# Flamingo layer pair on one core: broadcast one-hots for the expert map, paired base adds without an awaited store, head normalisation on ScalarE and 16-bit gate selection

## What is computed

```python
# second block ("ffn"): 16 heads of width 64, 8 experts, two chosen for each token and head
w, sel = top_k(x @ Ws, 2); mix_v = sigmoid(w) on the chosen experts
v = mix_v * (x @ Wv);  attn = softmax(q k^T / 8) @ v
mask_o = one_hot(top_k(x @ Wd, 2)).sum();  out = einsum(mask_o, attn, Wo)
# fourth block ("moe"): 12 experts, three for each token
topw, sel = top_k(x @ Wg, 3);  cw = softmax(topw) on the chosen experts
h = gelu(x @ Wup[e] + bup[e]);  y = h @ Wdown[e] + bdown[e];  out = sum_e cw[e] * y[e]
```

## Time and profile before

| | us |
|---|---|
| median of 3 runs (lowest, highest) | 1533.5 (1526.81, 1538.6) |
| the profiled execution | 1535.35 |
| its span, first to last instruction | 1533.6 |
| `ffn_stage` in it | 305 to 821 |
| `route` in it | 1053.3 to 1133.3 |
| `run_experts` in it | 1133.3 to 1533.6 |

### The profile page before, as it was taken

The page is one execution under the profiler, slowest core; times in us unless marked ns, Lnnn a source line. Parts: engine busy times, 40 slices in busy tenths (PEclk is TensorE's granted clock), DMA queues, the critical chain, the costliest instruction groups (busy, mean ns, idle before and its releaser), DMA issues. The chain is left out here.

```text
span 1533.6 us, 35189 instructions
## 1 busy us (share of the span) xinstructions
PE 1313.0 (86%) x13822; PEld 1029.4 (67%) x13822; DVE 1180.1 (77%) x2235; ACT 853.8 (56%) x1815; POOL 276.9 (18%) x240
## 2 busy tenths in 40 slices
PE   2399999768898898998975999995379999999997
PEld 2266767546676676776753667764258899989996
DVE  2656767568999999999863577776949888888884
ACT  1256666325565555555641666664227676767672
POOL 2000000000000000000000000000015666666663
PEclk9958788579999999999976899995569999999999
DMA  7000000023424334335321000000548888888771
GB/s 217 11 5 9 5 5 2 1 52 80 125 72 111 107 87 115 87 85 136 94 61 33 8 6 9 1 1 2 171 136 251 235 242 237 242 237 238 232 210 31
DMA packets 172065, 152.96 MB, mean 100 GB/s; under 512 B 62589, under 2 KB 154386, under 8 KB 171906
## 3 DMA queue, kind: packets, MB, share of 16 engines
q1 hardware_dynamic: 151906, 129.51, 28.4%
q0 software_dynamic: 13936, 16.79, 5.7%
q10 hardware_dynamic: 6064, 4.46, 1.0%
HBM read 116.89 MB, written 36.70 MB: 100 GB/s over the span
## 5 line engine op out<-in xcount | busy, mean ns | idle before, releaser
L1826 POOL DMA_INDIRECT out<-m_yo,m_xg x70 | 161.1, 2301 | 138.2 <-DVE m_yo L1941 122.7
L1848 ACT ACTIVATE m_hf<-m_ps,m_bue 128x256 f32<-128x256 f32 x280 | 117.2, 471 | 106.5 <-PE m_ps L84 106.5
L1051 ACT ACTIVATE f_pr<-f_ps,f_nb 128x256 f32<-128x256 f32 x256 | 107.1, 472 | 104.3 <-DVE f_nb L1314 99.7
L82 PE MATMUL m_ps<-m_xt,m_us 128*128 128x256 f16 x560 | 153.8, 275 | 0.0
L83 PE MATMUL m_ps<-m_xt,m_us 128*128 128x256 f16 x560 | 153.7, 274 | 0.0
L84 PE MATMUL m_ps<-m_xt,m_us 128*128 128x256 f16 x560 | 153.7, 274 | 0.0
L82 PE MATMUL m_ps<-m_ds,m_hs 128*128 128x256 f16 x560 | 152.6, 273 | 0.3 <-DVE m_yo L1941 0.3
L84 PE MATMUL m_ps<-m_ds,m_hs 128*128 128x256 f16 x560 | 152.6, 273 | 0.0
L83 PE MATMUL m_ps<-m_ds,m_hs 128*128 128x256 f16 x560 | 152.6, 273 | 0.0
L690 DVE SCALAR_TENSOR_TENSOR x_pt<-x_ps,x_pt 120x512 f16<-120x512 f32 x128 | 88.3, 690 | 77.7 <-ACT x_pt L480 77.0
L472 ACT ACTIVATE x_pr<-x_ps,x_mx 128x120 f32<-128x120 f32 x512 | 142.8, 374 | 8.3 <-DVE x_mx L686 8.3
(11 more groups left out here) (364 smaller groups left out, 3894.3 us busy)
## 6 DMA issues: line engine op xcount, KB each, us to landing
m_uraw<-in_L_ffn_Wup SPq DMA_DIRECT2D x35, 1024.0 KB, 5.4
m_draw<-in_L_ffn_Wdown SPq DMA_DIRECT2D x35, 1024.0 KB, 5.6
head_values<-f_v_row SPq DMA_DIRECT2D x16, 520.0 KB, 5.4
f_vh<-head_values SPq DMA_DIRECT2D x16, 520.0 KB, 3.8
head_outputs<-f_at_row SPq DMA_DIRECT2D x16, 512.0 KB, 3.0
f_at_in_t<-head_outputs SPq DMA_DIRECT2D x16, 512.0 KB, 6.0
expert_values<-f_pv_row SPq DMA_DIRECT2D x8, 512.0 KB, 2.8
f_pv_in_t<-expert_values SPq DMA_DIRECT2D x8, 512.0 KB, 5.6
```

What stands on the lines that cost most here:

```text
L82: pe.matmul(out, lhs[0], rhs[0], start=(n == 0), stop=False)
L1051: ins = act.activation(pr[h % 2][:, ti, :], S(h)[:, ti, :], ACT.Exp, bias=nb[h % 2][:, ti:ti + 1])
L1826: pool.indirect_dma_start(rows_of, bass.IndirectOffsetOnAxis(xg[j % RING][:, ti, D:D + 1].bitcast(I32), 0), yo[j % 2][:, ti, :], None, bou ...
L1848: ins = act.activation(hf[:, q, m, :], U(q)[:, m, :], ACT.Gelu, bias=weights.bue[par][:, 2 * q + m:2 * q + m + 1], scale=UNSPLIT)
```

## The change

In `ffn_stage` the multiplication of `normalise` goes from VectorE, where it is one instruction for a pair of heads, to ScalarE, where it is four Copy activations of 128 x 64 with the reciprocal as scale, behind `exps` in the same odd step; VectorE keeps the reciprocal and signals `rs_done`. The tensors `hit` and `sel` become 16-bit, the second maximum has a 16-bit tensor `top_rank` of its own, and the ranks are copied once into 16 bits (`rank16`).

In `route` the 16-bit identity is made first, and the transposes wait for it alone; the running sum takes four shifted additions of all 12 experts; the three `picked` products become one; the one-hots are made by three groups of three broadcast instructions, whose last dimension is a pair, so that lanes, columns and row numbers are stored twice over; TensorE waits for a group of 16 choices; the base is made for two tiles at a time over four banks, with eight additions of 128 x 512 for sixteen of 128 x 256; and SyncE no longer waits for the store of the base.

```diff
@@ ffn_stage
-        hit = sb("hit", [P, TPB * GATES, E0])
-        sel = sb("sel", [P, TPB, 2, H, E0])
+        hit = sb("hit", [P, TPB * GATES, E0], F16)
+        sel = sb("sel", [P, TPB, 2, H, E0], F16)
+        rank16 = sb("rank16", [P, E0], F16)
...
+            def normalise(b, hp):
+                h = 2 * hp
+                act.wait_ge(rs_done, H // 2 * b + hp + 1)
+                for i in range(2):
+                    h8, x = at_head(h + i)
+                    for ti in range(TPB):
+                        ins = act.activation(at[:, ti, h8, x, :], O(h)[:, i, ti, 0:DH], ACT.Copy,
+                                             scale=rs[hp % 2][:, 2 * i + ti:2 * i + ti + 1])
+                ins.then_inc(o_done, 1)
...
                     if b < B:
                         exps(b, h)
+                    if h % 2 == 1:
+                        if h >= 5 and b < B:
+                            normalise(b, (h - 5) // 2)
+                        elif h < 5 and b >= 1:
+                            normalise(b - 1, (h - 5) // 2 + H // 2)
...
-                ranks = bcast_mid(s.rank[:, E1 - E0:E1], TPB * GATES)
+                ranks = bcast_mid(rank16[:], TPB * GATES)
...
-                chain(dve.reciprocal(r, O(h)[:, :, :, DH]))
-                dve.tensor_tensor(at[:, :, h8:h8 + 2, x, :].rearrange("p t h d -> p h t d"), O(h)[:, :, :, 0:DH],
-                                  r.unsqueeze(3).to_broadcast([P, 2, TPB, DH]), ALU.mult).then_inc(o_done, 1)
+                dve.reciprocal(r, O(h)[:, :, :, DH]).then_inc(rs_done, 1)
@@ route
+            chain(pool.tensor_copy(ident16[:], s.ident[:]))
             pool.memset(ones[:], 1.0)
...
-            sp.wait_ge(b_done, TILES)
+            sp.wait_ge(b_done, B)
             sp.dma_start(out.rearrange("b (t p) d -> p (b t) d", p=P), s.x[:]).then_inc(out_based, 16)
-            sp.wait_ge(out_based, 16)
...
-            pe.wait_ge(masks_made, 6)
+            pe.wait_ge(masks_made, 1)
...
-            for tile in range(TILES):
-                if tile % 4 == 0:
-                    pe.wait_ge(cwt_done, tile // 4 + 1)
-                if tile >= 2:
-                    pe.wait_ge(b_done, tile - 1)
-                pe.matmul(BASE(tile), cwt[:, tile * P:(tile + 1) * P], s.bdown[:],
-                          start=True, stop=True).then_inc(b_ready, 1)
+            for q in range(B):
+                if q % 2 == 0:
+                    pe.wait_ge(cwt_done, q // 2 + 1)
+                if q >= 4:
+                    pe.wait_ge(b_done, q - 3)
+                for ti in range(TPB):
+                    tile = TPB * q + ti
+                    last = pe.matmul(BASE(q)[:, ti, :], cwt[:, tile * P:(tile + 1) * P], s.bdown[:], start=True, stop=True)
+                last.then_inc(b_ready, 1)
...
-            chain(dve.tensor_copy(ends[:, 0:1], blocks[:, 0:1]))
-            for e in range(1, E1):
-                chain(dve.tensor_tensor(ends[:, e:e + 1], ends[:, e - 1:e], blocks[:, e:e + 1], ALU.add))
+            chain(dve.tensor_copy(sums[1][:, SHIFT:], blocks[:]))
+            for i, back in enumerate((1, 2, 4, 8)):
+                chain(dve.tensor_tensor(sums[i % 2][:, SHIFT:], sums[1 - i % 2][:, SHIFT:],
+                                        sums[1 - i % 2][:, SHIFT - back:SHIFT + E1 - back], ALU.add))
...
-            for n in range(CHOICES):
-                dve.tensor_scalar(lane_hot[:, n, :], lanes[:], lane_f[:, n:n + 1], None, ALU.is_equal)
-                ins = dve.tensor_scalar(column_hot[:, n, :], lanes[:, 0:COLUMNS], column_f[:, n:n + 1],
-                                        row_f[:, n % TILES:n % TILES + 1], ALU.is_equal, ALU.mult)
-                if n % HOT_GROUP == HOT_GROUP - 1:
-                    ins.then_inc(hot_ready, 1)
+            spread = lambda ap, k: ap.unsqueeze(2).to_broadcast([P, TILES, k, 2])
+            counting = lambda k: lanes[:, 0:2 * k].rearrange("p (k d) -> p k d", d=2).unsqueeze(1).to_broadcast([P, TILES, k, 2])
+            for r in range(TOP1):
+                group = slice(r * TILES, (r + 1) * TILES)
+                into = column_hot[:, group, :].rearrange("p n (k d) -> p n k d", d=2)
+                chain(dve.tensor_tensor(into, counting(COLUMNS // 2), spread(column_2[:, group, :], COLUMNS // 2), ALU.is_equal))
+                dve.tensor_tensor(lane_hot[:, group, :].rearrange("p n (k d) -> p n k d", d=2),
+                                  counting(P // 2), spread(lane_2[:, group, :], P // 2), ALU.is_equal)
+                dve.tensor_tensor(into, into, spread(row_2[:], COLUMNS // 2), ALU.mult).then_inc(hot_ready, 1)
...
-            for tile in range(TILES):
-                dve.wait_ge(b_ready, tile + 1)
-                dve.tensor_tensor(s.x[:, tile, :], s.x[:, tile, :], BASE(tile), ALU.add).then_inc(b_done, 1)
+            for q in range(B):
+                pair = slice(TPB * q, TPB * q + TPB)
+                dve.wait_ge(b_ready, q + 1)
+                dve.tensor_tensor(s.x[:, pair, :], s.x[:, pair, :], BASE(q), ALU.add).then_inc(b_done, 1)
```

More of the change, by code:

```diff
@@ L1346, in _ @@
             dve.wait_ge(made, 6)
+            chain(dve.tensor_copy(rank16[:], s.rank[:, E1 - E0:E1]))
             for j in range(FF_FRONT - 1):
@@ L1542, in route @@
         sb = lambda name, shape, dt=F32: prep.enter_context(nc.sbuf_tensor(t + name, shape, dt))
+        two = lambda name, shape, dt=F32: [sb(f"{name}{i}", shape, dt) for i in range(2)]
         xn = sb("xn", [P, TILES, WIDE])
@@ L1555, in route @@
         top = sb("top", [P, 3, TILES])
-        filled, blocks, ends = sb("filled", [P, E1], I32), sb("blocks", [P, E1]), sb("ends", [P, E1])
-        start = sb("start", [P, E1])
+        filled, blocks, sums = sb("filled", [P, E1], I32), sb("blocks", [P, E1]), two("sums", [P, SHIFT + E1])
+        ends, start = sums[1][:, SHIFT:SHIFT + E1], sb("start", [P, E1])
         slot_f, slot_i = sb("slot_f", [P, CHOICES]), sb("slot_i", [P, CHOICES], I32)
         lane_i, column_i = sb("lane_i", [P, CHOICES], I32), sb("column_i", [P, CHOICES], I32)
-        lane_f, column_f = sb("lane_f", [P, CHOICES]), sb("column_f", [P, CHOICES])
+        lane_2, column_2 = (sb(n, [P, CHOICES, 2], F16) for n in ("lane_2", "column_2"))
         lanes_i, lanes = sb("lanes_i", [P, P], I32), sb("lanes", [P, P], F16)
-        row_i, row_f = sb("row_i", [P, TILES], I32), sb("row_f", [P, TILES])
+        row_i, row_2 = sb("row_i", [P, TILES], I32), sb("row_2", [P, TILES, 2], F16)
         lane_hot = sb("lane_hot", [P, CHOICES, P], F16)
@@ L1584, in _ @@
             chain(pool.iota(lanes_i[:], [[1, P]], base=0, channel_multiplier=0))
-            pool.tensor_copy(row_f[:], row_i[:])
+            pool.tensor_copy(row_2[:], bcast(row_i[:], 2))
             chain(pool.tensor_copy(lanes[:], lanes_i[:]))
-            chain(pool.tensor_copy(ident16[:], s.ident[:]))
             pool.iota(nth[:], [[1, NB]], base=0, channel_multiplier=0)
             pool.memset(xn[:, :, D + META:WIDE], 0.0)
+            for i in range(2):
+                pool.memset(sums[i][:, 0:SHIFT], 0.0)
             pool.iota(token[:], [[P, TILES]], base=0, channel_multiplier=1)
@@ L1741, in _ @@
             chain(dve.tensor_copy(blocks[:], filled[:]))
[L1742 to L1745 removed]
+            chain(dve.tensor_copy(sums[1][:, SHIFT:], blocks[:]))
+            for i, back in enumerate((1, 2, 4, 8)):
+                chain(dve.tensor_tensor(sums[i % 2][:, SHIFT:], sums[1 - i % 2][:, SHIFT:],
+                                        sums[1 - i % 2][:, SHIFT - back:SHIFT + E1 - back], ALU.add))
+            chain(dve.tensor_tensor(start[:], ends, blocks[:], ALU.subtract))
             chain(dve.scalar_tensor_tensor(place[:], bcast_mid(start[:], TILES), float(BT), RANK, ALU.mult, ALU.add))
[L1747 to L1748 removed]
+            chain(dve.tensor_tensor(picked[:].rearrange("p r t e -> p r (t e)"), chosen[:].rearrange("p r t e -> p r (t e)"),
+                                    bcast_mid(place[:].rearrange("p t e -> p (t e)"), TOP1), ALU.mult))
             chain(dve.tensor_reduce(slot_f[:], picked[:].rearrange("p r t e -> p (r t) e"), AX_X, ALU.add))
```

43 lines of the change are left out of this document (20 added, 23 removed).

## The result

The changed kernel takes 1484.61 us in the median (1481.57 to 1492.49, 4 runs) against 1530.15 us of the kernel before on the same chip: a ratio of 0.9706, with a 95% interval of 0.9641 to 0.9772. The forecast was 1491 us, faster: 42.4 us less than before, where the medians here are 45.5 apart. The profiled execution took 1487.02 us, with a span of 1485.3 us, 48.3 us less than the span before.

What follows compares the result with a forecast made beforehand. VectorE was taken to bound seven elements of `ffn_stage`, and `route` to be a chain; 22.4 us from `route` plus 20 from `ffn_stage`, 42.4 in all, took the median from 1533.5 to 1491 us, range 1472 to 1512.

Steps and rivals of the forecast that it cites:

- The rival in which TensorE takes over: `ffn_stage`: TensorE becomes the limit, only heavy steps give, some 8 us left there, 1503 us in all; chance 0.14.
- the one in which ScalarE paces every odd step: `ffn_stage`: `normalise` on ScalarE delays `pt_part` and TensorE in odd steps; 19 us slower, 1552 us; chance 0.02.
- First transposes: `route`: with the identity made first, TensorE's transposes start earlier, -1.1 us.
- Running sum: `route`: a copy and four additions instead of a copy and 11, 1.0 us for 2.3, -1.3.
- Products: `route`: three products of 192 values become one of 576, 0.76 us, -0.4; twice-stored lanes and columns give 0.1 back.
- One-hots: `route`: 96 VectorE instructions of 17.9 us become three groups of 2.6, 7.8 in all, -10.1 us.
- More products behind the last group: `route`: TensorE has 16 products left behind the last one-hot group instead of 8, +0.5 us.
- Base: `route`: four banks let TensorE go on, -2.1 us; the wider last addition costs 0.3; together -1.8.
- Store: End of `route`: without SyncE's wait for the base's store the experts start 8.3 us earlier, 0.5 left for the barrier.
- Store ordering: Experts: block 2's weights queue behind the store; cost 0, up to 8.3 us if late, rival 1499 us, chance 0.08.
- `ffn_stage`: Moved multiplication and 16-bit gates relieve VectorE of 4.3 us an element; 2.9 come through, times seven, 20 us; drain 0.
- Comparisons in 16 bits: `ffn_stage`: two comparisons of 16-bit ranks with one broadcast value gain 0; by the other reading 4 us more.

Runs made afterwards that it cites:

- e3: The changed kernel with SyncE's wait for the base's store put back; 1489.76 us, ratio 0.9751.
- e7: The changed kernel with a second 2 MB store, into a tensor nothing reads, behind the base's in SyncE's queue; 1487.66 us, ratio 0.9776.
- e4: The changed kernel with the 96 single one-hot instructions and groups of eight back; 1491.62 us, ratio 0.9754.
- e8: The changed kernel with four of eight base products ahead of the map's, six banks, and four additions ahead of VectorE's first weight split; 1482.68 us, ratio 0.9726.
- e2: The changed kernel with the multiplication of the heads back on VectorE, 16-bit gates kept; 1490.39 us, ratio 0.9759.
- e10: e5 with the heads of the last batch element alone normalised on VectorE; 1476.52 us, ratio 0.9662.
- e9: e8 with mask spreads one step later as in e5 and the third block's gathers moved from `route` to the experts' stage; 1469.53 us, ratio 0.9632.
- e6: The changed kernel with each of the four activations of a pair made twice on ScalarE, the copy never read; 1495.23 us, ratio 0.9795.
- e5: The changed kernel with VectorE's two mask spreads in steps 8 and 9 instead of 7 and 8; 1478.81 us, ratio 0.9708.

## Why the prediction was right

**The bound.** That VectorE paces the full elements held: relieved of 4.3 us it gave 3.29, and it is still the fullest engine. The rival in which TensorE takes over (8 us of gain in the stage) fell; the stage gave 20.6. So did the one in which ScalarE paces every odd step: one step in an element gave back 0.37 us.

**First transposes,** -1.1: they now start 2.67 us after the stage's first instruction instead of 3.43, so -0.8, and VectorE's halves release them. **Running sum,** -1.3: from its copy to `start` 1.02 instead of 2.33, -1.3. **Products,** -0.4: 0.79 instead of 1.18 us, -0.4; the doubled lanes and columns cost 0.04, not 0.1. **One-hots,** -10.1: 7.75 instead of 17.9, -10.1. **More products behind the last group,** +0.5: 1.21 us of waiting instead of 0.74, +0.5. The map's copy came at 42.3 us instead of 54.4, -12.1 against -12.3.

**Base,** -1.8: from the map's copy to the store's issue 14.67 instead of 16.93, -2.3. The 32 products took 14.02 us in one piece, 0.44 each, at the clock of 0.50 that the earlier trace rows had; more of them in a row did not raise it. **Store,** -8.3: 1.45 instead of 9.17, -7.7, and 6.96 in e3. This is the term that was a little too large: I left 0.5 us for the handover, and it is 1.45, so the sign that the first block comes within 1 us of the store's issue was missed. `route` as a whole: -22.0 against -22.4.

**Store ordering,** 0: no DMA wait at block 2's split. I had called it a draw at 12 us, and the load landed 10.5 us after the first block, 0.6 us before ScalarE wanted it. The forecast's limit was too late: in e7 the split at 15.0 us already costs 2.9, so the cost begins nearer 12.

**`ffn_stage`,** -20: -20.6, in part by luck, and by another road in three places. Of the light steps with a pair of heads, 9, 11 and 13 let all of VectorE's gain through (0.47, 0.48 and 0.48 us shorter), 15 and 1 a part (0.13 and 0.34), and only step 10, which follows `normalise`, gave back 0.37, of which 0.35 is VectorE's wait for `pt_part`, the delay forecast at 0.15 to 0.5.

```profile
536.66 0.69 DVE L1334 SCALAR_TENSOR_TENSOR f_pt<-f_ps,f_pt 128x512 f16<-128x512 f32 x1 [0.35 <-ACT f_pt L1022]
```

Step 7, where 0.43 was to come through whole, gave nothing because of GpSimd, which I had not looked for. And the element's 2.9 was to count seven times; in fact 3.29 counts in five full elements (16.4 us), the first gave 1.7, the second 0, and the last element with its drain 3.0, which I had at 0; the first projections took 0.5 more. The errors cancel: 0.4 too little an element, two elements too many, and nothing for the end. The 0 of the second element is chance as well: TensorE was granted 1.00 there before and 0.93 in this execution, and in e3, e4, e7 and e8, granted 1.00, the same code took 47.8 us instead of 50.5, so 2.7 less. Their whole stage took 493.0 to 493.3 us (e8: 495.8) where this execution's took 496.1, so the change is worth up to 23.7 us here, and the term of 20 was a little small.

**Comparisons in 16 bits, and the engine for the multiplication.** That a comparison with one broadcast value gains nothing from 16 bits held: L1256 and L1264 took 687 and 693 ns in the median, while the products with the ranks and the addition, whose operands all run with step one, fell from 692 to 425. With this the page "VectorE: DVE Perf Modes" of the Trainium skill (section What auto-detection actually checks) agrees. The rule of the page "ScalarE: Activation LUTs" of the Trainium skill (section Rules for kernel authors), to multiply on VectorE rather than on ScalarE, agrees on the single price, 0.94 us against 0.42, and was wrong as advice in the full elements: e2, which follows it there, has an element 2.5 us longer, since VectorE is the engine that is never free. Behind them it holds: e10, which follows it in the last element alone, is 0.9 us shorter there than e9.

## What to carry to other kernels

Where one engine is never free, price an instruction by what the loop gives when it leaves, not by its own length: four activations of 0.94 us in all, on an engine with room, beat one instruction of 0.42 on the full one, by 2.5 us for eight pairs, and lose 0.9 where the other engine has time. Many small instructions with a scalar per partition can become one broadcast instruction, and in 16 bits with a last dimension of two the broadcast took 1.23 us for 2048 values, where comparisons with a plain broadcast value took 0.69 for 512. And a wait that leaves the end of a stage only pays as far as the next thing that the end waits for: look which other queue, GpSimd's gathers here by all signs, is late next.

## What the runs showed of the hardware

The mask spread, a VectorE instruction that reads two tensors, takes longer beside GpSimd's subtraction: 1.70 or 1.71 instead of 1.22 us for 128 x 2048 in 16 bits, wherever they overlap by 0.62 or 0.63 us in the change, e3 and e6, and 1.22 again once they are apart (e5). The page "SBUF — State Buffer" of the Trainium skill (section Terms) says that the two engines take turns at a shared port pair and that the loser waits for the whole instruction; the runs agree in part: in the change the loss is 0.48 us for 0.63 of overlap, as if VectorE had stood still for most of it, but the 0.14 us of overlap before cost next to nothing. Both fit a full stop that ends some 0.15 us ahead of GpSimd's recorded end; that is an estimate from these two cases, which no run tests.

GpSimd's issue of a gather in `route`, 0.95 us as a rule, took 1.79 us in the change and 1.97 in e8 and e9 where VectorE's split of weights, also of two tensors, and an addition lay beside it, and 2.85 us once in e9, at the start of the experts, beside 2.0 us of a split. But the first gather of the change lay beside a split for its whole length and took 1.06. No run was made to part the two.

TensorE stayed at a granted clock of 0.50 through 14.02 us of back-to-back 32-bit products with 12 rows, and was at 0.65 to 0.73 for 29 us around the last element in eleven executions of twelve, though busy for 26 of the 29 us.
